# Every third pass of the edge sweep gets its source rows from a table in SBUF, instead of 27 passes three and four apart

## What is computed

```python
# layer 0, a relational layer with attention: the only one that handles edge after edge
x, y = h[src], h[dst]                       # 100,000 rows of 32
c = w_comp[etype]                           # 16 factors of each edge
msg = einsum('eb,ebo->eo', c, einsum('ei,bio->ebo', x, weight))
x_hat = x @ A1_w.T + A1_b
y_hat = y @ A2_w.T + A2_b + rel_emb[etype]
a = tanh(relu(sum(x_hat * y_hat, -1) / sqrt(32)))
h_new = relu(segment_sum(a[:, None] * msg, dst) + h[src[last_e]] @ self_loop_weight)
x = layernorm(x + h_new)
x = layernorm(x + segment_sum(x[src], dst))             # layer 1
x = layernorm(x + edge_softmax_sum(x, attn_w))          # layer 2
x = layernorm(x + ten_propagation_steps(x))             # layer 3
```

## Time and profile before

| | |
|---|---|
| time, median of 3 runs | 1147.88 us (1146.41 to 1151.34) |
| the profiled execution | 1148.57 us, of which the span of its records is 1146.8 us |
| mean granted clock of TensorE | 0.878 |
| busy share of the span | DVE 81%, PE 77%, POOL 53%, ACT 44% |
| gathers issued by POOL | 568 (71 passes of 8 tiles) |
| one-hot tiles for picks on DVE | 189 (27 picks of 7) |
| first and second `products_of` of the sweep | at 70.45 and 75.46 us |
| first gather starts, last one ends | at 11.43 and 791.03 us |
| last `make_mixed` of the sweep | at 806.10 us |

### The profile page before, as it was taken

One profiled execution on the slowest core, in us unless ns is written; L12 is line 12 of the kernel. 1 busy time (PEld: TensorE's weight loads), 2 busy tenths in 40 slices (PEclk: granted clock), 3 DMA queues, 4 the chain that ended last, 5 costly groups with the idle time before them and its releaser, 6 DMA issues.

```text
span 1146.8 us, 56069 instructions
## 1 busy us (share of the span) xinstructions
PE 883.4 (77%) x23682; PEld 838.9 (73%) x23682; DVE 933.5 (81%) x2369; ACT 504.8 (44%) x1244; POOL 608.6 (53%) x580
## 2 busy tenths in 40 slices
PE   2358887978686868777867768688468958999996
PEld 2357877877686867776767667587467958999996
DVE  8869999998898989898888988798557995555556
ACT  1135555554454546566756566556567400000000
POOL 5777777777777777777777777774000000000000
PEclk9569999888888888888988897978578979999998
DMA  4432333332232333232323322320000000000001
GB/s 117 60 75 55 64 59 60 66 57 51 48 60 54 57 52 59 52 57 57 57 56 56 51 54 50 68 45 13 5 2 3 4 2 4 5 4 4 4 5 19
DMA packets 54917, 47.97 MB, mean 42 GB/s; under 512 B 35966, under 2 KB 45182, under 8 KB 54662
## 3 DMA queue, kind: packets, MB, share of 16 engines
q0 software_dynamic: 18176, 9.34, 10.3%
q1 hardware_dynamic: 30822, 14.16, 6.1%
q10 hardware_dynamic: 5664, 20.84, 4.9%
HBM read 41.98 MB, written 2.31 MB: 39 GB/s over the span
## 4 chain that ended last, share of the span: by engine, by line
POOL 42%; DVE 19%; PE 18%; issue 16%; DMA 2%; ACT 2%; DVEq 0%; SPq 0%; ACTq 0%
POOL arena L631 42%; PE ps L883 14%; DVE arena L1372 2%; DVE arena L1612 2%; PE ps L854 2%; PE ps L893 2%; DVE arena L1411 2%; DVE arena L1632 1%; ACT arena L1120 1%; DMA arena<-line_table 1%; DMA arena<-rel_rows_in 1%; DVE aggT L1424 1%; DVE arena L1362 1%; PE ps L816 1%; DVE arena L1387 0%
## 5 line engine op out<-in xcount | busy, mean ns | idle before, releaser
L631 POOL DMA_INDIRECT arena<-x_pad,arena x568 | 606.8, 1068 | 173.4 <-issue 172.5
L816 PE MATMUL ps<-aggT 128*128 128x128 f16 x3024 | 217.3, 238 | 1.6 <-DVE aggT L1424 1.3
L816 PEld LDWEIGHTS ps<-aggT 128*128 128x128 f16 x3024 | 205.6, 110 | 3.1 <-DVE aggT L1424 3.1
L1372 DVE TENSOR_SCALAR arena<-pair_no,arena 128x275 bf16<-128x275 f16 (+2 forms) x784 | 183.1, 292 | 0.0
L883 PE MATMUL ps<-arena,adj_words 128*128 128x64 f16 x5625 | 171.9, 192 | 3.4 <-DVEq L1697 3.2
L883 PEld LDWEIGHTS ps<-arena,adj_words 128*128 128x128 fp8e4 x5625 | 170.5, 97 | 4.7 <-DVEq L1697 3.6
L1411 DVE TENSOR_TENSOR arena<-ps,arena 128x1536 f32<-128x1536 f32 x98 | 171.6, 1751 | 0.6
L1073 ACT ACTIVATE adj_words<-arena 128x500 uint8 x196 | 126.5, 646 | 56.5 <-ACT arena L1048 54.2
L1043 ACT ACTIVATE arena<-ps 128x500 fp8e4<-128x500 f32 x196 | 113.0, 577 | 86.9 <-PE ps L765 86.7
L758 PE MATMUL ps<-arena 128*128 128x25 bf16 x195 | 36.5, 187 | 148.7 <-DVE arena L1372 148.3
L778 PE MATMUL ps<-arena 128*32 128x44 f32 (+4 forms) x7048 | 131.3, 212 | 17.6 <-DVE arena L1411 17.5
(11 more groups left out here) (221 smaller groups left out, 1160.6 us busy)
## 6 DMA issues: line engine op xcount, KB each, us to landing
arena<-line_table ACTq DMA_DIRECT2D x48, 344.0 KB
arena<-x_pad,arena POOLq DMA_INDIRECT x568
arena<-pick_table SPq DMA_DIRECT2D x27, 256.0 KB
arena<-line_table ACTq DMA_DIRECT2D x48, 80.0 KB
arena<-dst_parts SPq DMA_DIRECT2D x196, 5.7 KB
agg_table<-arena SPq DMA_DIRECT2D x196, 2.5 KB
dst_parts<-aggT SPq DMA_DIRECT2D x1, 735.0 KB, 12.7
x<-x_pad SPq DMA_DIRECT2D x1, 400.0 KB
```

Of the source, the lines that this page charges most:

```text
L631: pool.indirect_dma_start(to, None, table, bass.IndirectOffsetOnAxis(ap=index, axis=0)).then_inc(done, 16)
L816: mm = nc.tensor.matmul(ps[:, at:at + PICK_WIDE * FEAT], pick_hot[:, u % PICK_RING, k * P:(k + 1) * P], x_parts[:, t, j * PICK_WIDE:(j + 1 ...
L1372: last = v.tensor_scalar(pair_hot[:, d % 2, k, 0:n], pair_no[:, 0:n], pair_of[:, d * DUO + k // SLOTS, k % SLOTS:k % SLOTS + 1], None, ALU ...
```

## The change

The list of portions has one entry instead of two, and the places that used 2 for its length use its real length. Now every pick takes three passes (3, 2, 2 units). Picked passes are 5, 8, 11, ... 95 (31 of 98) in place of 6, 9, 13, 16, 20, ... 93, 97 (27 of 98). The last pass, which has 6 tiles, was picked before and is gathered now, so POOL issues 66 x 8 + 6 = 534 gathers instead of 568.

```diff
-PICK_UNITS = ((2, 2, 2, 1), (3, 2, 2))
+PICK_UNITS = ((3, 2, 2),)
 def pick_plan():
     starts, units, picked, at = [], {}, [], 1
-    while at + len(PICK_UNITS[len(picked) % 2]) + 1 < DUOS:
+    while at + len(PICK_UNITS[len(picked) % len(PICK_UNITS)]) + 1 < DUOS:
         c, deep = len(picked), 0
-        for d, n in enumerate(PICK_UNITS[c % 2]):
+        for d, n in enumerate(PICK_UNITS[c % len(PICK_UNITS)]):
             units[at + d] = [(c, j) for j in range(deep, deep + n)]
             deep += n
         starts.append(at)
-        at += len(PICK_UNITS[c % 2])
+        at += len(PICK_UNITS[c % len(PICK_UNITS)])
         picked.append(at + 1)
```

## The result

The changed kernel takes 1117.7 us (median of 4 runs, 1111.1 to 1123.4) against 1148.3 for the kernel before on the same chip: a ratio of 0.973, 95% interval 0.967 to 0.979, so 31 us less, give or take 7. A second set of five runs gave 1117.2 us, ratio 0.972 (0.970 to 0.974). The forecast was 1106 us with a range of 1095 to 1121. The direction and the range held; the gain was three quarters of the forecast one, and the time lies in the part of the range that the text gave to a rival.

What follows compares the result with a forecast made beforehand. POOL's gathers were taken to bound the sweep; with 34 fewer, POOL and DVE nearly balance, pass 97 is reached at 757.7 us and weigh comes 42.3 us earlier: 1148.6 - 42.3 = 1106.3, forecast 1106 us, range 1095 to 1121.

Steps and rivals of the forecast that it cites:

- What bounds before, and that the change moves it: POOL's gathers set the pace from about pass 26; moving work to DVE brings both within 1 us of balance.
- POOL's sum: Sweep: 34 gathers fewer take off 42.2 us, 1.2 us a pick adds 4.8; last gather ends at 753.6 us.
- DVE's own sum: Sweep: 4.9 us a pick, 19.5 for four; three-pass turns of 21.16 us, pass 97 at 746.7 without waits.
- The start of the sweep: Preparation: four mask instructions of twice the size instead of eight save 1 us; the sweep starts at 69.5 us.
- The waits for the tanh: DVE waiting for ACT's tanh: one 0.64 us wait in each of the last 17 turns, 11 us; pass 97 at 757.7.
- PE, ACT, SP at nothing: 448 more products on PE, ACT's work unchanged, four more SP loads of 256 KB: all costed at nothing.
- The end of the sweep: From products_of(96) to the tanh of pass 97: 11.0 us instead of 13.1; weigh at 763.5, 42.3 us earlier.
- DVE and ACT become the bound: Rival: waits for the tanh grow to 1.6 us in 17 turns, 27 us, 1122 us; half, 1114; chance 0.18.
- the main case: The forecast itself: 1106 us, with 11 us of waits for the tanh; 1100 to 1111, chance 0.60.
- Nothing extra: Rival: POOL done at 744.4 us, no waits for the tanh, weigh 53 us earlier, 1096 us; chance 0.10.
- held up in full: Rival: DVE's pick instructions hold up gathers for their whole length; last gather at 766.8 us, 1114 us; chance 0.08.
- PE did not take over: Rival, slower than before: at clock 0.65 a PE turn takes 25.4 us, 61 us more, 1209 us; chance 0.02.

Runs made afterwards that it cites:

- halved gathers: POOL issues 4 of 8 gathers a pass from pass 22 on: changed kernel 1115.1 us (0.969), kernel before 1094.5 us (0.950).
- both orders: Changed kernel, ACT takes the next pass's tanh before the piece and copies moved sums after the first copy of the counts: 1105.9 us, 0.962.
- 28 picks: Against the kernel before: 28 picks, two of three passes then one of four, and 558 gathers: 1143.7 us, ratio 0.994.
- 81 more units: Kernel before, with the second pick unit's one-hot tile made once more on DVE in 81 passes: 1151.0 us, ratio 1.001.
- one part: Changed kernel, each pick unit's products for the upper fp16 part of x only, 8 instead of 16 on PE: 1114.4 us, ratio 0.968.
- short piece: Changed kernel, ACT's count_piece adds up 8 columns instead of 1024: 1110.0 us, ratio 0.965.
- ACT reordered: Kernel before, next pass's tanh ahead of the piece and copy of moved sums behind the first copy of the counts: 1144.8 us, ratio 0.997.

## Why the prediction came out as it did

**What bounds before, and that the change moves it:** right. The waits for landings went from 51.9 us to 1.5, and the runs with halved gathers show both sums: before, 54.6 us could be had from POOL; after, 2 to 3.

**POOL's sum: direction right, mechanism not shown.** It ended at 761.65 us where 753.6 was forecast. The delays did stay when gathers went: 534 x (1.101 + 0.30) is 748, where the old mean would give 732. But the price per pick was 1.2 us by estimate, and no fixed price exists. Of POOL's sum, busy time and gaps together, the change took 29.1 us (780.2 to 751.1) where 37.4 were forecast, so that four picks added 13.1 us of delays and not 4.8. By the same sum they added 6.2 us in the run with both orders, and in the run with 28 picks one pick alone added 10.4, while at one place 81 more units left POOL alone. Which DVE instructions lie beside a gather goes with most of its length (the table above); what sets how the passes and the gathers come to lie was not found. The Trainium skill's rule ("SBUF — State Buffer", "Who interferes with whom") would give each repeated unit up to its full 0.48 us where a gather is under way; the run shows 0.02 on average, so by it alone the time can't be worked out.

**DVE's own sum: right.** 19.5 us for four picks were forecast, 19.0 measured. Turns were forecast at 21.16 us; of the 30 turns between the first and the last, the 14 without a wait took 20.97 to 21.52, 21.11 on average.

**The start of the sweep: wrong by 1.7 us.** One microsecond was to be saved in the preparation. The masks took 4 x 0.73 us (2.93) for 8 x 0.38 (3.04), and it would not have mattered: ahead of pass 0 DVE waits 9.3 us for a landing of the edge lines, 9.0 before. In all traces the sweep starts between 70.4 and 72.4 us, with either plan.

```profile
40.20 2.93 DVE L1307 TENSOR_SCALAR arena<-arena 128x248 f16<-128x248 int32 x4
...
70.51 0.75 DVE L1349 TENSOR_SCALAR arena<-arena,side_no 106x2048 bf16<-106x2048 bf16 x1 [9.29 <-DMA arena<-line_table]
71.18 0.42 DVE L1387 TENSOR_TENSOR arena<-ps,arena 128x264 f32<-128x264 f32 x1
```

**The waits for the tanh: the mechanism right, the size too small.** The forecast was 11 us, 17 waits of 0.64, all after pass 46. There were 21 of 0.67, 14.0 us, three of them before pass 46 (18, 30 and 42), besides 1.5 us for one landing. The reading behind it was wrong in one point: of the 14 waits before, one (0.47 us) stood in pass 28, and so the argument that none came before pass 46 did not hold.

**PE, ACT, SP at nothing: this step failed.** "ACT's work is unchanged" is true of its sum and says nothing of its order. Pass 97 was reached at 767.15 us instead of 757.7: 1.7 us from the start, 3.0 from the tanh, 1.5 from a landing, and 3.2 more. These 3.2 lie in the turns that have a wait: less their waits, the other 16 of those 30 took 21.39 us on average, 0.3 more than the 14 without. So the tanh's lateness costs more than the waits that the profile names; what the rest of it is was not looked into. The run with one part shows that PE's products for the picks have a share in the tanh's lateness, the short piece and the new order that ACT's queue is where it can be mended.

**The end of the sweep: right.** 11.0 us were forecast from `products_of(96)` to the tanh of pass 97 and 0.2 to `weigh`; from 761.90 to 773.42 are 11.5, against 13.3 before. Beyond the sweep another 1.2 us went the same way: the rest of the span takes 0.4 us longer, and 2.6 us lie outside the records where the forecast kept the 1.8 of before.

**The rivals.** "DVE and ACT become the bound" had 0.18 and a band of 1111 to 1122 us. The engines are the ones that it names, and the time lies in its band, but not by its sum: it had waits for the tanh of 19 to 27 us, and 14.0 is nearer to the 11 of the main case. The rest came from small terms that all erred the same way (start, landing, turns, end), so that the band was met is partly luck. "Nothing extra" and "held up in full" did not happen. PE did not take over: its granted clock was 0.90 from 75 to 765 us. The price of that rival was too low in any case: the 23.5 us for three passes hold only from pass 21 on, and over the whole sweep before it was 22.6, so a turn of 25.4 would have cost some 90 us and not 61.

## What to carry to other kernels

When work moves from one engine to another until both are as late, the time goes by the sum of the now later engine plus the waits that its spare time used to pay for; read those small waits in the profile before, since each of them will be on the path. An engine that is 45% busy can be on the path by the order of its queue: ask for each short instruction that others wait for what stands in front of it, and whether that could come behind. Taking the unwanted half of an engine's work away, in both kernels, gives the other engine's sum without an estimate, once the waits that are left or new in that run are taken off.

## What the runs showed of the hardware that had not been expected

An indirect gather of 128 rows took 1.06 to 1.10 us on average, with the same 0.94 at least, and the mean did not follow how much work DVE had. Before, it was 1.068 us; with ACT reordered 1.061, with 81 fp16 instructions more 1.071, with 81 fp32 adds more 1.068. With one pick more it was 1.090, with four 1.101 (1.103 in the second trace), and with four and ACT reordered 1.088. In the kernel before, a gather beside `make_rows` (two bf16 inputs in SBUF) took 1.332 us on average, and one beside none of the four instructions of the table 0.952.

The same eight products on PE took 1.03 us at a granted clock of 0.50 and 0.63 at 0.97 or more. Both times stand behind an idle stretch of about 2.4 us in one trace or the other, so that stretch alone does not decide it; no run settles what does.
